# PSUM operands for wide VectorE operations in two stages of a four-layer graph network, and three row scalings made row by row

## The reference

```python
x = layernorm(x + hyperbolic_attention(x, edges))   # L0
x = layernorm(x + ngcf_convolution(x, edges))       # L1, two convolutions
x = layernorm(x + attention_4_heads(x, edges))      # L2
x = layernorm(x + attention_with_edge_features(x, edges))  # L3
```

## Time and profile before

| | |
|---|---|
| median of three runs | 8034.38 us (8027.68 to 8039.57) |
| profiled execution, first to last instruction | 8027.0 us |
| DVE busy | 5509.6 us, 69% |
| POOL busy | 5303.4 us, 66% |
| PE busy, ACT busy | 2987.5 us, 2914.7 us |
| first attention layer | about 1385 to 2962 us of the span |
| last stage | about 7440 to 8027 us of the span |

### The profile page before, as it was taken

The page is one execution under the profiler, slowest core; times in us unless marked ns, Lnnn a source line. Parts: engine busy times, 40 slices in busy tenths (PEclk is TensorE's granted clock), DMA queues, the critical chain, the costliest instruction groups (busy, mean ns, idle before and its releaser), DMA issues. The chain is left out here.

```text
span 8027.0 us, 77025 instructions
## 1 busy us (share of the span) xinstructions
PE 2987.5 (37%) x14049; PEld 2387.9 (30%) x14049; DVE 5509.6 (69%) x16229; ACT 2914.7 (36%) x6536; POOL 5303.4 (66%) x5145
## 2 busy tenths in 40 slices
PE   4776700211111115766656635454400000263322
PEld 1222200211111115666646634454400000252221
DVE  6667687877767756777779969999734444473764
ACT  3555523433333334444435536666500000121211
POOL 0003773777777767777757737777567777777677
PEclk9888855555555557778856655555555555576555
DMA  9884218111111114555569944444321111663321
GB/s 101 110 117 98 68 18 63 27 26 26 26 25 25 25 39 141 168 163 167 160 212 327 328 159 148 146 151 151 126 62 44 45 45 45 132 226 114 97 91 61
DMA packets 786581, 864.04 MB, mean 108 GB/s; under 512 B 469875, under 2 KB 483427, under 8 KB 779804
## 3 DMA queue, kind: packets, MB, share of 16 engines
q1 hardware_dynamic: 572556, 684.47, 30.9%
q0 software_dynamic: 163408, 175.42, 10.5%
q10 hardware_dynamic: 50240, 0.60, 0.6%
HBM read 419.15 MB, written 480.23 MB: 112 GB/s over the span
## 5 line engine op out<-in xcount | busy, mean ns | idle before, releaser
L164 POOL DMA_INDIRECT T<-slot_at,home_row x393 | 434.4, 1105 | 818.4 <-DVE home_row L728 677.9
L1244 POOL DMA_INDIRECT e_other<-X,index x392 | 428.1, 1092 | 177.3 <-issue 117.4
L1232 POOL DMA_INDIRECT e_ahead<-XA,index x392 | 416.3, 1062 | 178.6 <-issue 118.8
L1892 POOL DMA_INDIRECT e_mine<-T,index x392 | 392.3, 1001 | 206.1 <-issue 114.3
L3012 POOL DMA_INDIRECT e_got<-G,index x392 | 411.6, 1050 | 176.7 <-issue 112.9
L3634 POOL DMA_INDIRECT out_rows<-e4s_out,index x392 | 416.8, 1063 | 165.2 <-issue 118.8
L2383 PE MATMUL e_turned<-ident,e_own_x 128*128 128x128 f32 x196 | 54.6, 434 | 1229.4 <-DVE e_own_x L1971 1229.4
L1904 POOL DMA_INDIRECT X<-e_row,index x392 | 419.0, 1069 | 125.3 <-issue 118.8
L2532 POOL DMA_INDIRECT e_got<-X,index x392 | 413.6, 1055 | 119.5 <-issue 119.5
L2529 POOL DMA_INDIRECT e_mine<-X,index x392 | 404.4, 1032 | 130.4 <-issue 119.2
L3443 POOL DMA_INDIRECT rows<-X,index x392 | 395.6, 1009 | 130.6 <-issue 130.6
(11 more groups left out here) (685 smaller groups left out, 13023.6 us busy)
## 6 DMA issues: line engine op xcount, KB each, us to landing
XA<-e_n_xa SPq DMA_DIRECT2D x49, 1056.0 KB, 5.5
SUMS<-e_state SPq DMA_DIRECT2D x49, 1056.0 KB
e4n_n_xa<-XA SPq DMA_DIRECT2D x49, 1056.0 KB, 5.3
X<-e_n_row SPq DMA_DIRECT2D x49, 576.0 KB
X<-pl_x SPq DMA_DIRECT2D x98, 268.0 KB, 3.0
e_n_x<-X SPq DMA_DIRECT2D x49, 536.0 KB
B<-e_n_b SPq DMA_DIRECT2D x49, 528.0 KB
e_n_b<-B SPq DMA_DIRECT2D x49, 528.0 KB
```

The source lines that it names most:

```text
L164: gp.indirect_dma_start(out=words, out_offset=bass.IndirectOffsetOnAxis(ap=home_row[:, t:t + 1], axis=0), in_=slot_at[:, t:t + 1], in_offs ...
L1232: gp.indirect_dma_start(out=ahead[:, b, j, :], out_offset=None, in_=g.XA[0:SLOTS, :], in_offset=bass.IndirectOffsetOnAxis(ap=index_of(g, 0 ...
L1244: gp.indirect_dma_start(out=other[:, h, j, :], out_offset=None, in_=others[:, :], in_offset=bass.IndirectOffsetOnAxis(ap=index_of(g, s, 1, ...
L1892: gp.indirect_dma_start(out=mine[:, h, j, :], out_offset=None, in_=g.T0[:, :], in_offset=bass.IndirectOffsetOnAxis(ap=index_of(g, s, 0, n, ...
```

## The change

Nothing is moved in the order of the instructions of any engine. Some tiles change their memory, three wide operations are each written as eight, and one ACT instruction is written as two.

In the first layer, `hp` becomes a PSUM tile called `scratch`; `t2` is written to it too (it was the second half of `big`), so the sum `ma` reads `big` from SBUF and `hp` from PSUM, and `y` reads `hp` from PSUM and `own_x` from SBUF. `own_x`, `other_x` and the scaled part of `row` were one `tensor_tensor` each with a repeated operand of 8 numbers per partition; they become eight `tensor_scalar` of 64 numbers, with one number per partition as the scalar, and no wait between the eight.

In the last stage the two blocks of `ex` that are multiplied with `rows` and `mine` go to a PSUM tile `rise`; `share`, `own_pay` and `y` become PSUM tiles; `y` has one buffer in place of two; `spread` and `carried` share a PSUM bank, `ends`. ACT's one exponential over 1176 numbers per partition becomes one over 392 in SBUF and one over 784 in PSUM.

```diff
-        big, squares = sb("big", [P, 2, J, D]), sb("squares", [P, J, D])
+        big, squares = sb("big", [P, J, D]), sb("squares", [P, J, D])
...
-        ... hp ... = ... sb("hp", [P, J, D]) ...
+        ... hp ... = ... ps("scratch", [P, J, D]) ...
...
-                    copied.done(v.tensor_tensor(own_x[:, h, :, :], mine[:, h, :, 0:D], mine[:, h, :, SHIFT:SHIFT + 1].to_broadcast([P, J, D]), ALU.add))
+                    for j in range(J):
+                        last = v.tensor_scalar(own_x[:, h, j, :], mine[:, h, j, 0:D], mine[:, h, j, SHIFT:SHIFT + 1], None, ALU.add)
+                    copied.done(last)
...
-                    copied.done(v.tensor_tensor(other_x[:, :, :], other[:, h, :, 0:D], other[:, h, :, SHIFT:SHIFT + 1].to_broadcast([P, J, D]), ALU.add))
+                    for j in range(J):
+                        last = v.tensor_scalar(other_x[:, j, :], other[:, h, j, 0:D], other[:, h, j, SHIFT:SHIFT + 1], None, ALU.add)
+                    copied.done(last)
...
-                    dve.done(v.tensor_tensor(big[:, 1, :, :], other_y[b][:, :, :], per(tmp[:, 10, :]), ALU.mult), "t2")
+                    dve.done(v.tensor_tensor(hp[:, :, :], other_y[b][:, :, :], per(tmp[:, 10, :]), ALU.mult), "t2")
                     need("t2")
-                    dve.done(v.tensor_tensor(big[:, 0, :, :], big[:, 0, :, :], big[:, 1, :, :], ALU.add), "ma")
+                    dve.done(v.tensor_tensor(big[:, :, :], big[:, :, :], hp[:, :, :], ALU.add), "ma")
...
-                    x1_made.done(v.tensor_tensor(row[:, h, 0:count, 0:D], y[:, b, 0:count, :], per(norm_t[:, b, 4, 0:count], count), ALU.mult))
+                    for j in range(count):
+                        last = v.tensor_scalar(row[:, h, j, 0:D], y[:, b, j, :], norm_t[:, b, 4, j:j + 1], None, ALU.mult)
+                    x1_made.done(last)
...
-        top, ex, gain, weight, share = sb("top", [P, T + 1]), sb("ex", [P, 3, T]), ..., sb("share", [P, T])
+        top, ex, gain, weight, share = sb("top", [P, T + 1]), sb("ex", [P, T]), ..., ps("share", [P, T])
...
-        pay, own_pay, state = sb("pay", [P, J, D]), sb("own_pay", [P, J, D]), sb("state", [P, RING, J, D])
+        pay, own_pay, state = sb("pay", [P, J, D]), ps("own_pay", [P, J, D]), sb("state", [P, RING, J, D])
...
-        p_t, y, squares, small = sb("p_t", [P, 4, P]), sb("y", [P, 2, J, D]), ...
+        p_t, y, squares, small = sb("p_t", [P, 4, P]), ps("y", [P, J, D]), ...
...
+        ends, rise = ps("ends", [P, P + D + 1]), ps("rise", [P, 2, 512])
+        own_rise, other_rise = rise[:, 1, 0:T], rise[:, 0, 0:T]
...
-                    acc.done(v.tensor_tensor(pay[:, :, :], g.rows[:, n * J:n * J + J, 2:], per(1), ALU.mult), "first")
+                    acc.done(v.tensor_tensor(pay[:, :, :], g.rows[:, n * J:n * J + J, 2:], per(other_rise), ALU.mult), "first")
...
-                    if begun(c, 2):
-                        v.wait_ge(out_made.sem, out_made.after(n - 2))
+                    if begun(c, 1):
+                        v.wait_ge(out_made.sem, out_made.after(n - 1))
...
-                prep_act.done(a.activation(ex[:, :, :], ex[:, :, :], ACT.Exp), "ex")
+                a.activation(ex[:, :], ex[:, :], ACT.Exp)
+                prep_act.done(a.activation(rise[:, :, 0:T], rise[:, :, 0:T], ACT.Exp), "ex")
```

More of the change, by code:

```diff
@@ L1986, in products @@
                         v.wait_ge(dve.sem, dve.after(n - 1, "rise"))
[L1987 removed]
+                    dve.done(v.tensor_tensor(big[:, :, :], own_row_y[:, :, :], other_y[b][:, :, :], ALU.mult), "prod")
                     need("prod")
[L1989 removed]
+                    v.tensor_reduce(tmp[:, 0, :], big[:, :, :], AX.X, ALU.add)
                     v.wait_ge(gathered[h], (c.k + 1) * 32 * J)
@@ L3765, in running_sums @@
                             need(f"run{j - 1}")
-                        acc.done(v.scalar_tensor_tensor(out=state[:, h, j, :], in0=before, scalar=ex[:, 0, n * J + j:n * J + j + 1],
+                        acc.done(v.scalar_tensor_tensor(out=state[:, h, j, :], in0=before, scalar=ex[:, n * J + j:n * J + j + 1],
                                                         in1=pay[:, j, :], op0=ALU.mult, op1=ALU.add), f"run{j}")
@@ L3779, in y_rows @@
                     v.wait_ge(kept_act.sem, kept_act.after(n))
-                    if begun(c, 2):
-                        v.wait_ge(out_made.sem, out_made.after(n - 2))
-                    y_made.done(v.tensor_tensor(y[:, b, 0:count, :], result[:, 0:count, :], kept[:, b, 0:count, :], ALU.add))
+                    if begun(c, 1):
+                        v.wait_ge(out_made.sem, out_made.after(n - 1))
+                    y_made.done(v.tensor_tensor(y[:, 0:count, :], result[:, 0:count, :], kept[:, b, 0:count, :], ALU.add))
                 def norm(c, count):
@@ L3802, in out_slots @@
                     v.wait_ge(filed[h], c.k * 16 * J)
-                    out_made.done(v.tensor_tensor(out[:, h, :, :], y[:, b, :, :], small[:, 3, :].unsqueeze(2).to_broadcast([P, J, D]), ALU.mult))
+                    out_made.done(v.tensor_tensor(out[:, h, :, :], y[:, :, :], small[:, 3, :].unsqueeze(2).to_broadcast([P, J, D]), ALU.mult))
                 attention()
@@ L3818, in _ @@
                 v.wait_ge(rooted.sem, rooted.after(NCH))
-                v.tensor_scalar(fixed[:, :], y[:, FIX.slot % 2, 0, :], small[:, 3, 0:1], None, ALU.mult).then_inc(fixed_made, 1)
+                v.tensor_scalar(fixed[:, :], y[:, 0, :], small[:, 3, 0:1], None, ALU.mult).then_inc(fixed_made, 1)
             @block.scalar
@@ L3859, in squares_of @@
                         a.wait_ge(square_sum.sem, square_sum.after(n - 1, "sum"))
-                    squared.done(a.activation(squares[:, 0:count, :], y[:, b, 0:count, :], ACT.Square))
+                    squared.done(a.activation(squares[:, 0:count, :], y[:, 0:count, :], ACT.Square))
                 def roots(c, count):
@@ L3885, in body @@
                         pe.wait_ge(fix_act.sem, fix_act.after(0, "rise"))
-                        fix_pe.done(pe.transpose(spread[:, :], rises[:, :], g.ident[:, :]), "turned")
+                        fix_pe.done(pe.transpose(spread, rises[:, :], g.ident[:, :]), "turned")
                     if c[2] and c[2].n == 4:
@@ L3910, in _ @@
                 pe.wait_ge(fix_dve.sem, fix_dve.after(0, "diag"))
-                fix_pe.done(pe.matmul(spread[:, :], lhsT=g.ones[:, :], rhs=diag[:, :], start=True, stop=True), "spread")
+                fix_pe.done(pe.matmul(spread, lhsT=g.ones[:, :], rhs=diag[:, :], start=True, stop=True), "spread")
                 unrolled(NCH, SKEW, body)
```

34 lines of the change are left out of this document (17 added, 17 removed).

## The result

The changed kernel takes 7960.58 us (median of four runs, 7954.37 to 7962.95); the kernel before, run beside it on the same chip, 8033.76; the forecast was 7988. The ratio is 0.9911, 95% interval 0.9897 to 0.9925: 73 us faster, where the forecast said 46.

What follows compares the result with a forecast made beforehand. POOL's own string of transfers was taken to bound both stages. Gains of 33 us (last stage) and 13 (first layer: 34 less 15 less 6) take the 8027.0 us span to 7981; 7 more gives 7988 us, range 7966 to 8026.

Steps and rivals of the forecast that it cites:

- What bounds the kernel: Both stages: POOL's own string of transfers is their length; transfers starting during wide two-SBUF DVE operations wait for them.
- Last stage: Last stage: 35.8 us over the floor, less 2 for running sums and 0.5 for a second exponential, so 33 gained.
- First layer, what goes and what stays: First layer: four lines' holds of 35.1 us go, 34 counted; hp, pay, t1, att, elu and centring stay as summed.
- First layer, what comes: First layer: 24 tensor_scalar rows a round, 0.16 us apart, each holding a transfer half a row; 15 us lost.
- The third rival: First layer: rows of 64 hold POOL not at all; 7973 us, chance 14%.
- The tail: First layer after the last gather: DVE's chain sets the pace, so rows add 4 us, 6 with POOL in the way.
- The offset: Whole kernel: the timed median stands 7 us above the profiled span, added to 7981.
- The first: First layer: groups of rows hold POOL as one operation, 139 us over 42 rounds; 8112 us, chance 7%.
- The second: First layer: rows cost 0.29 us each, 30 us of waits and 12 in the tail; 8009 us, chance 15%.
- The fourth: Last stage: DVE or the landing of scatters takes POOL's place, its gain is nothing; 8021 us, chance 3%.
- The first rival's threshold: First layer: holds by groups of rows eat both stages' gains from about 1.8 us a round on.
- the forecast's own range: Whole kernel: 7978 to 8001 us, with 28 to 36 in the last stage and rows at 0 to 20; chance 61%.

Runs made afterwards that it cites:

- one_scalar_wide: The whole change, but the three scalings as one tensor_scalar of 512 numbers each instead of eight rows; 7984.92 us, ratio 0.9934 to the kernel before.
- rows_two_waits: The whole change, with rows as tensor_tensor with two SBUF inputs and a wait between the sixteen rows of shifted; 7974.85 us, 0.9917 to the kernel before.
- rows_doubled: The whole change, with each of the sixteen rows of shifted made twice, the extra into a spare tile; 7965.68 us, 0.9910 to the kernel before.
- last_only: The kernel before with only the last stage's part of the change, the first layer as before; 8003.66 us, ratio 0.9954 to the kernel before.

## Why the prediction was right or wrong

**What bounds the kernel: right.** POOL's string of transfers is the length of both stages (but for the tail of the first), DVE's wide two-SBUF operations lengthen it, and one PSUM operand ends that. All three hold in every run above, and in a stage (the node stage) that the prediction did not look at. They are not the whole: a wide operation with one SBUF operand holds POOL too (one_scalar_wide), and two-SBUF rows with gaps do not (rows_two_waits).

**Last stage: right.** 33 us forecast, 35.5 in the trace, 35.6 with this part alone. The allowance of 2 us for the running sums and 0.5 for the second exponential was not needed: the scatters are over their floor by under 1 us in all, and from the end of the last gather to the first scatter, where the exponentials lie, it is 46.2 us after 46.1.

**First layer, what goes and what stays: right in sum.** The lines that kept two SBUF operands, the running sums among them, held 38 us before and 39 after. The prediction took that sum as it is. Each share moved, though: `hp` fell from 13.6 to 0.3 us, `att` rose from 4.1 to 12.7. As the prediction said, the sum of `ma` (now line 2019) holds no transfer, and `y` (now 2180) holds 0.1 us. That the sum of the rest held was luck and no rule; with other edits single lines rose by far (`elu` from 6.0 to 12.1, `n_out` from 1.5 to 21.5), and in rows_doubled the sum is 5 us less.

**First layer, what comes: wrong, and this is the step that failed.** The prediction said: "a transfer waits for the row under way", half a row, 0.08 us, in some 3 transfers a round, doubled to 15 us. The count was about right (185 in 49 rounds, 3.8 a round), and the pitch too, from the start of one row to that of the next (0.163 us against 0.16). The wait of each was wrong: 0.010 us, no more than beside an idle DVE. So the rows hold POOL by 2 us at the most instead of 15, and the gathers are 31 us shorter instead of 19. Line 1974 had been read as a sign that POOL gets in between two operations; the step still charged it for half of each one. The third rival had this mechanism right, at 14%.

**The tail: wrong in the same direction.** 6 us were forecast, 1.2 measured. last_only, which has no rows, has the same 116.0 us, so even 1.2 can't be told from what two traces differ by. The prediction took DVE's chain of rounds for what sets the tail. But POOL's waits for DVE's `row` there rose from 6.5 us to 8.6 only, over three scatters; the others follow at POOL's own pace, as before. Part of the rows' time also took the place of waits of DVE itself, for ACT's results: on line 2166 (old number) they add up to 4.6 us in four, on the same line of the changed kernel to 2.3 in three. The prediction said "The tail has no such cover", meaning the waits for gathers; it has others. DVE's two rows, from the stretch of the tail in the trace before and after:

```profile
DVE e_ball_t L2166 <- ACT e_ball_t L2341: 4.6, 4, 1.6
```

```profile
DVE e_ball_t L2170 <- ACT e_ball_t L2347: 2.3, 3, 0.9
```

**The offset.** The forecast added 7 us to the span, because the median stood that far above the profiled execution before. After, the median and the span are equal (7960.6 and 7960.3). The 27.4 us between the forecast and the result are then: 12.2 at the gathers, 4.8 in the tail, 2.5 in the last stage, 1.2 in unchanged stages, 6.7 in this offset. The last two of these are no more than what single executions differ by. With the rows at 2 us and the tail at 1.2 the forecast would have been 7970, inside the range. The range did not reach low enough for the third rival with a better last stage and a smaller offset, which all fell on the same side.

**The rivals.** The first, that a group of rows holds POOL as one, is false for these rows and true for rows with two SBUF operands, where it costs 37 us. The second is refuted by the pitch of 0.163 us. The fourth is refuted by the last stage's own length.

**Two sums.** Two sums of the prediction don't come out of its own terms. The first rival's threshold is put at 1.8 us a round, but 34 and 33 less 6, over 42 rounds, is 1.5. And the forecast's own range, with 28 to 36 us in the last stage and rows at 0 to 20, is 7970 to 7998, not 7978 to 8001. Neither moves the forecast, nor takes the result in.

## What to carry to other kernels

Where POOL issues transfer after transfer, look for the transfers that take longer than the shortest, and see which DVE operation each starts in. In these runs the wide ones with two SBUF operands are the ones that cost, and a repeated operand of a few numbers per partition, moved to PSUM, takes the cost away without a change of the order. Change all of the wide operations of a stage at once, since a stage with one left can pay nearly all of it there. Where PSUM is not to be had, one-operand rows of 64 numbers do the same, as long as DVE has time to give: eight of them take 1.4 us where one wide operation took 0.69.

## What was not expected of the hardware

- Rows of two SBUF operands that follow each other after 0.135 us hold a transfer that starts behind their first 0.33 us until 0.11 us before the last of them ends, up to 2562 ns for a scatter of 972; with 0.26 us between their starts they hold it by 13 ns on average.
- One-operand rows of 64 numbers, 0.163 us apart, do not hold POOL; one operation of 512 does, 286 ns at the most.
- The effect goes the other way too. Rows that start 0.5 to 0.6 us into a transfer of 0.94 take 467 ns at the median and end 0.02 us behind the transfer's end; some take up to 509 and 522 ns instead of 248 and 247. Rows that start in a transfer's first 0.4 us take no longer than usual. Yet the rows' starts stay 0.163 us apart, and the group of eight keeps its 1.4 us:

```profile
L1972 DVE TENSOR_SCALAR e_own_x<-e_mine x392: 236/248/509, 1400.2 to 2820.8; 128x64 f32<-128x64 f32 x196
L1977 DVE TENSOR_SCALAR e_other_x<-e_other x392: 233/247/522, 1401.5 to 2822.1; 128x64 f32<-128x64 f32 x196
```
